# Scores of two heads in tiles of 64 positions each, for heads 8 to 91 of an adaLN attention block

## The reference

```python
h = layernorm(x) * (1 + ca) + sa
q = h @ Wq.T                      # 32 heads of 128
k, v                              # 8 groups, each serves 4 heads; v and part of k through a low rank
q = q * cos + rotate_half(q) * sin
scores = einsum('bhqd,bhkd->bhqk', q, k) * scale
scores = where(causal, scores, -1e9)
attn = softmax(scores)
x = x + ga * (einsum('bhqk,bhkd->bhqd', attn, v) @ Wo.T)
h = layernorm(x) * (1 + cb) + sb
# a router softmax over 64 experts, the top 8 weights, a mix of 64 bias rows
x = x + gb * (h * w_sum + w_dense @ expert_bias)
```

## Time and profile before

| what | value |
|---|---|
| median of the runs | 1457.65 us |
| the profiled execution | 1456.07 us |
| its span | 1454.8 us |
| TensorE busy | 1430.2 us, 98% |
| VectorE, GpSimd, ScalarE busy | 79%, 70%, 69% |
| DMA engines, mean busy share | 74% |

### The profile page before, as it was taken

The page is one execution under the profiler, slowest core; times in us unless marked ns, Lnnn a source line. Parts: engine busy times, 40 slices in busy tenths (PEclk is TensorE's granted clock), DMA queues, the critical chain, the costliest instruction groups (busy, mean ns, idle before and its releaser), DMA issues.

```text
span 1454.8 us, 24655 instructions
## 1 busy us (share of the span) xinstructions
PE 1430.2 (98%) x7150; PEld 1207.3 (83%) x7150; DVE 1151.6 (79%) x3542; ACT 1009.3 (69%) x2391; POOL 1024.4 (70%) x805
## 2 busy tenths in 40 slices
PE   7999999999999999999999999999999999999998
PEld 7877888888888888888888888888888888888886
DVE  5687777787777777777777777777779988998876
ACT  5677666766676676767676677677677677776674
POOL 3767766776676677767676777677588888887662
PEclk9999999999999999999999999999999999999999
DMA  8478766775677767676677667659888899889972
GB/s 302 164 220 245 218 203 184 237 231 163 201 226 207 193 218 229 189 208 203 180 223 228 219 181 206 202 181 250 232 240 259 271 297 256 280 257 279 268 230 72
DMA packets 215157, 322.03 MB, mean 221 GB/s; under 512 B 42512, under 2 KB 132464, under 8 KB 215024
## 3 DMA queue, kind: packets, MB, share of 16 engines
q1 hardware_dynamic: 214736, 320.39, 73.8%
q10 hardware_dynamic: 288, 0.07, 0.0%
HBM read 179.43 MB, written 140.95 MB: 220 GB/s over the span
## 4 chain that ended last, share of the span: by engine, by line
PE 87%; DVE 4%; DMA 2%; POOL 2%; ACT 2%; issue 2%; SPq 1%; DVEq 0%; ACTq 0%
PE bank_s L638 22%; PE bank_o L794 22%; PE bank_pv L755 14%; PE bank_s L704 13%; PE bank_s L670 5%; PE bank_s L655 5%; PE bank_s L700 1%; PE bank_s L611 1%; POOL PT_lo L1851 1%; DMA blocks<-blocks 1%; PE bank_s L858 1%; DVE y L1557 1%; DVE blocks L1505 1%; PE bank_s L701 0%; DMA wc_scratch<-wc_out 0%
## 5 line engine op out<-in xcount | busy, mean ns | idle before, releaser
L1851 POOL TENSOR_TENSOR PT_lo<-PT_raw,PT_hi 128x640 fp32r<-128x640 f32 x246 | 383.9, 1584 | 32.4 <-ACT PT_hi L1142 32.4
L1128 ACT ACTIVATE probs<-probs,row_inv 128x512 f32<-128x512 f32 (+3 forms) x512 | 257.8, 553 | 192.1 <-DVE row_inv L1488 191.9
L1839 POOL TENSOR_TENSOR rot_c<-rot_c,rot_s 128x512 f32<-128x512 f32 x128 | 168.0, 1312 | 254.4 <-DVE rot_s L1445 254.3
L1121 ACT ACTIVATE probs<-probs,row_min 128x384 f32<-128x384 f32 (+3 forms) x512 | 281.5, 552 | 48.8 <-DVE row_min L1481 48.7
L1505 DVE STREAM_TRANSPOSE blocks<-probs 128x384 f32<-128x384 f32 x508 | 213.9, 446 | 21.9 <-ACT probs L1128 14.1
L704 PE MATMUL bank_s<-kT_both,qT_hi 128*128 128x512 f32 (+2 forms) x768 | 214.5, 340 | 4.7 <-issue 2.4
L1481 DVE CUSTOM_DVE_ANT_0 probs<-bank_s,mask 128x512 f32<-128x512 f32 (+2 forms) x384 | 205.3, 552 | 0.4
L1844 POOL TENSOR_TENSOR qT_lo<-rot_c,qT_hi 128x512 fp32r<-128x512 f32 x128 | 167.3, 1307 | 49.4 <-ACT qT_hi L1103 48.7
L638 PE MATMUL bank_s<-hT_lo,wq_hi 128*128 128x512 f32 x484 | 194.9, 403 | 1.9 <-DVE row_min L1481 1.4
L794 PE MATMUL bank_o<-wo_lo,OT_hi 128*128 128x512 f32 x496 | 195.0, 393 | 0.3 <-DVE rot_s L1445 0.3
L794 PE MATMUL bank_o<-wo_hi,OT_hi 128*128 128x512 f32 x496 | 193.4, 390 | 0.0
(11 more groups left out here) (311 smaller groups left out, 3190.3 us busy)
## 6 DMA issues: line engine op xcount, KB each, us to landing
blocks<-blocks SPq DMA_DIRECT2D x127, 640.0 KB, 3.8
PT_raw<-blocks SPq DMA_DIRECT2D x500, 160.0 KB, 3.9
stage<-in_wq SPq DMA_DIRECT2D x32, 256.0 KB, 5.2
vblocks<-kv_raw SPq DMA_DIRECT2D x32, 256.0 KB, 5.3
kv_raw<-vblocks SPq DMA_DIRECT2D x128, 64.0 KB, 2.2
stage<-in_wo SPq DMA_DIRECT2D x32, 256.0 KB, 5.2
split_wq<-wq_hi SPq DMA_DIRECT2D x32, 256.0 KB, 5.4
split_wq<-wq_lo SPq DMA_DIRECT2D x32, 256.0 KB, 5.7
```

What stands on the lines that cost most here:

```text
L1121: ins = act.activation(row(t, qt), row(t, qt), ACT.Exp, bias=row_min[m][:, qt:qt + 1], scale=-1.0, accum_out=row_sum[m][:, qt:qt + 1])
L1128: ins = act.activation(row(t, qt), row(t, qt), ACT.Copy, scale=row_inv[t % 2][:, qt:qt + 1])
L1839: pool.tensor_tensor(rot_c[:], rot_c[:], rot_s[:], ALU.add).then_inc(pool_a, 1)
L1851: pool.tensor_tensor(lo[:, at], raw_of(t)[:, at], hi[:, at].bitcast(F32), ALU.subtract).then_inc(pool_t, 1)
```

## The change

From head 8 to head 91 the heads are scored in pairs (8, 9), (10, 11) and so on. Both heads of a pair belong to one unit and share its keys. A score tile still has 128 rows, but they are 64 positions of both heads, interleaved (row 2x+h is position x of head h). Step t of the odd head takes the lower 64 positions of each 128, the step of the even head the upper 64. A tile of the odd step (`narrow`) needs 64 keys less: 448, 320, 192 and 64 columns instead of 512, 384, 256 and 128. Widths on DVE and ACT stay as they are; a second mask hides the 64 columns left over, and is loaded before head 8 and taken out before head 92.

Since both heads' queries are needed before the first scores of a pair, queries are projected four steps ahead instead of three: step 6 projects heads 9 and 10, steps 7 to 87 head t+4, step 88 none. `rot` gets room for two heads; the sine part of the odd head goes to `turned`, which lies under a low part of queries. The copies and subtractions that split the queries write every second element of `qT` (8 bytes apart), and the splits of the values' bank read every second element. The values' matmuls write their bank in runs of 32 columns.

The diff, cut to its core:

```diff
-CHUNKS = ["wo0", "wo1", "wo2", "wo3", "wk", "wq0", "wq1", "wq2", "wv", "wq3"]
+CHUNKS = ["wo0", "wo1", "wo2", "wo3", "wk", "wq0", "wq1", "wq2", "wq3", "wv"]
+HALF_TILE = P // 2
+MIXED_FROM, MIXED_TO = 8, (AGAIN - SHARED + 1) * GROUP + 4
+AHEAD_TO = MIXED_TO - 4
+BOTH_STEP = MIXED_FROM - 2
+EXTRA = MIXED_FROM + 2
+def projected(t):
+    ahead = [3, 4] if t == BOTH_STEP else [4] if BOTH_STEP < t < AHEAD_TO else [] if t == AHEAD_TO else [3]
+    return [t + n for n in ahead if t + n < ALL]
...
+        def in_row(w, t):
+            if two_heads(t):
+                return w.rearrange("p (q x h) -> p h q x", q=QT, h=2)
+            return w
+        def rotated(t):
+            if two_heads(t):
+                return rot_of(t)[:].rearrange("p h (q r x) -> p h q r x", r=2, x=HALF_TILE)[:, :, :, 1 - t % 2, :]
+            return rotated_head(t)
...
 (TensorE, scores)
-                    keys = (qt + 1) * P
+                    keys = (qt + 1) * P - (HALF_TILE if narrow(t) else 0)
 (TensorE, values)
-                to = pair_bank(p, tiles)[:].rearrange("p (i k) -> p i k", i=2 * SUBS)
+                to = pair_bank(p, tiles)[:].rearrange("p (q i a) -> p i q a", q=2, a=SUB)
 (TensorE, step)
-                if 2 < t < ALL - 3:
-                    q_proj(t + 3)
+                for q in projected(t):
+                    q_proj(q)
 (ScalarE, step)
+                if h % 2 == 0 and BOTH_STEP < t <= AHEAD_TO:
+                    q_split(t + 3)
...
 (VectorE, step)
+                sums_first = h % 2 == 0 and BOTH_STEP < t <= AHEAD_TO
+                if sums_first:
+                    invert_sums(t + 1, 1)
+                for q in projected(t):
+                    if q != EXTRA:
+                        q_rope(q)
+                if not sums_first:
+                    invert_sums(t + 1, 1)
...
 (GpSimd, even step)
+                    if BOTH_STEP < t <= AHEAD_TO:
+                        q_split(t + 3)
+                        split_moved_lo(t - 1, [0])
+                        if h == 2:
+                            k_rope(u + 1)
+                        split_moved_lo(t - 1, [1])
+                        if h == 2:
+                            k_split(u + 1)
...
+                    for q in projected(t):
+                        q_rope(q)
+                        if t == BOTH_STEP and q != EXTRA:
+                            q_split(t + 2)
+                            q_split(t + 3)
```

More of the change, by code:

```diff
@@ L89, with two_heads, narrow, query_step @@
 LATE_SPLITS = 6
+HALF_TILE = P // 2
[3 more added lines that the diff above has]
+EXTRA = MIXED_FROM + 2
+def two_heads(t):
+    return MIXED_FROM <= t < MIXED_TO
+def narrow(t):
+    return two_heads(t) and t % 2 == 1
+def query_step(t):
+    return t - 4 if EXTRA <= t < MIXED_TO else t - 3
+def projected(t):
+    ahead = [3, 4] if t == BOTH_STEP else [4] if BOTH_STEP < t < AHEAD_TO else [] if t == AHEAD_TO else [3]
+    return [t + n for n in ahead if t + n < ALL]
+def queries_read(t):
+    return max([0] + [q + 1 for n in range(max(t - 1, 0)) for q in projected(n)])
 def q_offset(qt):
@@ L176, in build @@
         sin_t = whole.take("sin_t", [P, SEQ])
-        mask = whole.take("mask", [P, SEQ])
+        mask = whole.take("mask", [P, SEQ + HALF_TILE])
         y_at = whole.at
@@ L217, in build @@
         probs_end = whole.at
+        turned = Region(whole.at + 4 * SEQ).take("turned", [P, SEQ])
         qT = [[whole.take(f"qT_{p}{i}", [P, SEQ], F32R) for p in ("hi", "lo")] for i in range(2)]
@@ L234, in build @@
         small_end = whole.at
-        minus_half = whole.take("minus_half", [P, 1])
         assert whole.at <= nc.sbuf_usable_end
@@ L377, in place_of @@
         def place_of(t):
[L378 removed]
+            n = 1 - t % 2 if two_heads(t) else t % 2
+            return slice(n * CAUSAL, (n + 1) * CAUSAL)
         def parts_of(t):
@@ L628, in q_proj @@
                     pe.wait_ge(dve_h, BATCH * CH - 2)
-                elif t > 0:
+                elif t > 0 and t != EXTRA:
                     pe.wait_ge(dve_r, t)
                 if t > 6:
-                    pe.wait_ge(dve_s, score_read(t - 2, tile_order(t - 2)[0]))
+                    now = query_step(t) + 1 if t != EXTRA else BOTH_STEP + 1
+                    pe.wait_ge(dve_s, score_read(now, 2 if t == EXTRA else tile_order(now)[0]))
                 if t == GROUP * (SHARED - 1):
@@ L1221, in step @@
                     pair_split_hi(t // 2 - 2, LOWER)
-                if h % 2 == 1 and t + 2 < ALL:
+                if h % 2 == 1 and t + 2 < ALL and not two_heads(t + 2):
                     q_split(t + 2)
@@ L1468, in mask_and_max @@
                 m = t % 2
+                first = SEQ + HALF_TILE if narrow(t) else SEQ
                 if half == 0 and 0 < t <= BY_PE:
                     dve.wait_ge(dve_tp, t)
+                if half == 0 and t in (MIXED_FROM, MIXED_TO):
+                    dve.wait_ge(d_const, 80 if t == MIXED_FROM else 96)
                 for qt in half_order(t, half):
@@ L1475, in mask_and_max @@
                     if qt == 1:
-                        dve.tensor_tensor(row(t, 0), low_keys_bank, mask[:, SEQ - P:], ALU.add).then_inc(dve_low, 1)
+                        dve.tensor_tensor(row(t, 0), low_keys_bank, mask[:, first - P:first], ALU.add).then_inc(dve_low, 1)
                     if qt == 0:
@@ L1935, in step @@
                         ffn_gate(early(before))
-                    if t + 2 < ALL:
+                    if t + 2 < ALL and not two_heads(t + 2):
                         q_split(t + 2)
```

139 lines of the change are left out of this document (86 added, 53 removed).

## The result

The changed kernel takes 1458.49 us (median of 20 runs, 1456.53 to 1461.1), the kernel before 1456.58 us in the same comparison: ratio 1.0016, 95% interval 1.0009 to 1.0022. It is slower by 1.9 us in the medians and by 2.3 by the ratio, where I had forecast 2.7 us faster. The time lies inside my range of 8 in 10 (1448.5 to 1461.5), but on the other side of no change. The profiled executions agree: span 1457.3 us against 1454.8.

A forecast was written before the change was run, and what follows sets the result against it. TensorE, busy for 98% of the span, was taken to bound the kernel. Units' -3.4 us and the ends' +0.7 gave -2.7 us: 1457.65 - 2.7 = 1454.9 us, with an 8 in 10 range of 1448.5 to 1461.5.

The forecast's parts named there:

- two gates: Waits of TensorE: projection for the first tile's mask read, next unit's scores for the keys' low part at h = 2's end.
- part 2: Query projection waits for VectorE's mask read of the first tile: gain 0.25 us in h = 0, 0.08 in h = 2.
- part 3: GpSimd's fuller row delays the keys' low part: h = 2 becomes 0.07 us longer, -0.18 us per unit, -3.4 for 19.
- the second gate: Next unit's scores wait for GpSimd's keys' low part at the end of h = 2, starting 0.10 us behind it.
- Part 5: The two ends: step 6 +1.96 us, steps 7 to 10 +0.15, step 88 -1.3, step 90 -0.1; together +0.7.
- part 4: Other moves in the same steps (copies, rotations, weight pieces, mask loads) cost nothing; odd steps' scores unchanged.
- part 6: Steps of two elements in query and values' bank splits, and matmul writes in runs of 32 columns, cost nothing.
- Rival A: Slower: GpSimd's low parts of queries cost more with the step of two; a quarter more gives 1466.7 us; 12%.
- Rival C: Slower: odd steps' handing over of the values' bank, read with the step of two; 1.7 to 23 us; 8%.
- Rival B: Faster: GpSimd's row runs 0.15 us shorter, leaving only the mask wait in h = 2; 1452.0 us; 22%.
- 13.4 us of columns: TensorE's saving at most: 768 columns, 0.32 us, in each of 42 narrow steps.

The follow-up runs named there:

- experiment 1: The changed kernel with the odd heads' scores at full width again: 1463.45 us, ratio 1.0049 to the kernel before.
- experiment 5: The changed kernel, but in a unit's first score tile the product reading the keys' low part comes last and alone waits: 1453.65 us, ratio 0.9979.
- experiment 6: The changed kernel, with the smaller tile scored first in h = 2 and the keys' rotation ahead of three transposes in h = 1: 1460.29 us, ratio 1.0024.
- experiment 10: The kernel of experiment 8 with the odd heads' scores at full width again: 1459.11 us, ratio 1.0019.
- experiment 4: The kernel before, with the first half of the keys' low part made twice on GpSimd in steps h = 2 of 10 to 86: 1467.59 us, ratio 1.0075.
- experiment 9: The kernel before, with the keys' low part read last in every unit's first tile as the only edit: 1455.67 us, ratio 0.9995.
- experiment 2: The changed kernel, but VectorE instead of GpSimd makes the keys' low part in steps h = 2 of 8 to 87: 1470.93 us, ratio 1.0125.
- experiment 7: The changed kernel with the edits of experiment 5 and experiment 6 together: 1450.86 us, ratio 0.9957.
- experiment 3: The changed kernel, but VectorE inverts both halves' sums ahead of the rotation in odd steps too: 1455.05 us, ratio 0.9992.
- experiment 8: The changed kernel with the edits of experiment 5, experiment 6 and experiment 3 together: 1448.74 us, ratio 0.9946.

## Why the prediction was wrong

The direction was wrong: -2.7 us forecast, +2.5 of span measured, 5.2 apart. The mechanism, two gates behind which most of the columns are lost, was right (part 2 and part 3: experiments 1, 5, 6 and 10). The step that failed is the price of the second gate in part 3: +0.07 us a unit and nothing behind it, where the steps h = 2 and h = 3 measured +0.24 us a unit (+4.6 for +1.3). Two smaller terms went the same way.

- **Part 3, what the gate costs behind itself (+1.2 us).** I had read that scores start 0.10 behind the low part, and set the step behind it to nothing. TensorE's restart costs 0.08 more: the next matmul starts 0.30 to 0.31 instead of 0.23 behind, and h = 3 is up to 11.16. It could have been read in the trace of before: the second matmul behind step 10's wait at 181.99, 0.30 behind rows 8, and step 11 with 11.16. Experiments 4 and 5 show that it belongs to the wait: it comes with one in the kernel before and goes with it in the changed one.
- **Part 3, the room that was used up (+2.1 us in h = 2).** I took one unit's row for all. Part 3 says that GpSimd works without a gap, and I did not draw the conclusion that a DMA landing 0.3 late then moves the unit's end by 0.3: before, the slack of 0.40 would have taken it up. Five steps with +2.0 us together, four of them by late loads, one by a late mask, are most of the excess; the other 14 gave 0.10 instead of 0.07. The slack is not the whole account. Three profiled executions of the kernel before (with experiments 4 and 9) have late loads in one of these 19 units each, and where experiment 4 had used up the slack they cost 0.3 us. The changed kernel has them in four units, and the executions of experiments 1, 2, 5, 6 and 7 in two to five. So with the change more loads are late, and I had not thought of that; whether the change causes it, and how, was not tried. Steps 22 and 78 are among them in most executions.
- **Part 5, the two ends (+1.2 us).** Up to step 12 +2.69 for +2.1: the low part of head 8's queries, behind which step 6 ends, came 0.5 later than I had it (scores at 141.24 for 140.75); step 88 -0.97 for -1.3, its last third at 7.86 for 7.56; the steps from 93 on +0.22. Most of this item is scatter: in the executions of experiments 1, 2, 3 and 6, with nearly the same code there, steps 6 to 11 cost 1.8 to 2.4 us over the kernel before, around my 2.1, and the start of step 6 differs by up to 0.9 us.
- **Part 2, h = 0 (+0.6 us).** The projection starts at 1.51, forecast 1.49 (the release took 0.18 for 0.15), and the gain is 0.23 for 0.25; step 16 lost 0.33 to a late mask.
- **Parts 4 and 6 held, nearly.** Odd steps h = 1 are 11.08 and `OT_lo` takes 0.69 as before. The step of two is not quite free: in steps 12 to 88 `qT_lo` takes 1324 ns for 1309, 0.03 us in each unit's row and so part of the 0.10 above, and ScalarE's copy `qT_hi` 663 ns for 622, which stood at no gate. Rivals A and C did not come. The rule of the Trainium skill, "GPSIMD Engine Reference", section "Performance pitfalls for Q7 kernels", that a step of up to 8 bytes costs nothing extra is borne out to 1%. The sentence of "PSUM — Partial Sum Buffer", "Specifications", in the Trainium skill, that any non-contiguous pattern slows matmuls significantly, does not show at runs of 32 columns: values of 512 columns start 0.23 us apart and those of 256 columns 0.12, as before.
- **Rival B** (the second gate isn't there) is what experiment 5 builds: 9.76, as that rival had it.

The forecast was also a small difference of large terms: 13.4 us of columns against two gates. A miss of 0.1 us in each of 19 units is 2 us, nearly as much as the whole forecast. That all four misses went the same way is in part chance, since the ends alone scatter by up to a microsecond.

The change itself was worth more than the changed kernel shows: behind three small edits the kernel is some 8 us faster than before (experiment 8). With full columns that kernel takes 10.4 us more and is 2.7 slower than the kernel before (experiment 10): the columns are worth 10.4 there, and the ends and the new order of work cost 2.7 even with the three edits. Only the first of the edits was tried in the kernel before (experiment 9). The projection waits in steps h = 2 of the kernel before as well, so how much the other two would give there without the change is open.

## What to carry to other kernels

When an engine's row loses its last gap, price it by its worst unit and not by a clean one: a late DMA is then paid in full, there may be more late ones than before, and each wait of TensorE costs a restart behind it. Before taking work from the bound engine, list what stands right behind it (here 0.32 us of columns met gates at 0.08 and below nothing), and look for the operand that is late but can be read last: reordering three products of one tile gave back 4.6 us in steps h = 2 and h = 3. A second gate hides what the first one is worth, so test them together as well as alone.
